# A graph network with layer norm: the norm of four blocks in three turns, and the transposes of a block two turns later

## The chip, the cores and the metric

The kernel runs on one core of a Trainium2 chip. The metric is the device time of one execution in microseconds (us). Three runs of the kernel before gave 4486.59, 4495.84 and 4501.65 us; their median, 4495.84 us, is the time before.

## The reference, cut to what matters

There are 6250 nodes with 256 features and 106,250 edges, sorted by target node (50,000 in both directions, and a loop at each node). Four layers follow each other, each with a layer norm ahead and a residual sum behind:

```
h = LN(x);  h = h + segsum(h[src]);  h = relu(relu(h@W1a+b1a)@W1b+b1b)        # 256 -> 512 -> 512
h = h + segsum(h[src]);  x1 = x + relu(h@W2a+b2a)@W2b+b2b                      # 512 -> 256
x2 = x1 + slice_attention(LN(x1))       # softmax over 64 slices of 8 heads, tokens, attention, back
x3 = x2 + relu(batchnorm(segsum(norm * (LN(x2)@W)[src])))
out = x3 + moe_top2_of_8(LN(x3))
```

`segsum` sums over the edges of each target. All is float32.

## The kernel before

The nodes lie in 49 blocks of 128. Six stages follow one another, each with a barrier between: s0 sorts the edges into tiles and makes the first table, **s1**, **s2** and **s4** are the three that gather (first aggregation with W1a, W1b and W2a; second aggregation with W2b, the layer norm of x1, logits, softmax and token sums; third aggregation with its product, the layer norm of x3, gates and the placing of tokens to experts), s3 is the attention and s5 the experts. The change is in s1, s2 and s4.

In a gathering stage, the edges of a block are tiles of 128, three tiles to a **group**; four blocks have 23 groups (6, 6, 6 and 5), the stage 282 groups and 846 tiles. For each tile GpSimd (POOL) issues one indirect DMA (`Edges.gather`, L280) that fetches 128 rows of a table into a ring of groups: 8 slots in s1, 6 in s2 and s4. Ahead of a group's first gather it waits until TensorE (PE) has counted up `s_used` for the group that held the slot. VectorE (DVE) makes a 128x128 one-hot matrix for each tile (`Edges.onehots`, L295), six groups ahead. PE multiplies the one-hots with the gathered rows and sums up in one of two PSUM banks (`Edges.sums`, L320, and L330 for tiles that belong to two blocks).

Around this each engine walks the same list, `pipeline`. The blocks are cut into **supers** of four (eleven of them, then 2, 2 and 1 blocks). A **turn** is one group. `close(b)` ends a block: DVE adds the block's own rows to the PSUM sum into `agg` (L962, L1188, L1804), in the first turn of the next block (`close_first`); PE transposes `agg` (L990, L1266, L1907), and ScalarE (ACT) copies the transposes (L905, L1133, L1722), both in turn 1 (the second) of the next block. The dense work of a finished super is cut into 22 steps, `piece(s, k)`, that lie beside the turns of the next super: step k is put into turn 2 + k*(n-2)//22 of n turns. In a super of 23 turns these are turns 2, 2, 3, 4, ..., 22. Within a turn the order is: the group's work, `begin`, `close`, and the steps.

Steps touched in s2: products with W2b in steps 0 to 3 (`SECOND`, L1278, added to x1 by DVE at L1198), the layer norm in step 4 (`NORM`, L1202 to L1213, all on DVE: bias, statistics, a reciprocal root of 14 short chained instructions in `rsqrt`, L179 to L185, and four scalings), the transposes of the normed rows in steps 7 to 10 (`TURNED`, PE L1285; ACT copies each at L1141), logits in steps 8 to 11 (L1291), softmax in steps 12 and 13, and transposes and token sums in steps 17 to 20 (`SLICED`, L1298, L1302). In s4: products in 0 to 3 (L1920, L1824), norm in 4 (L1828 to L1838), transposes in 7 to 10 (L1929, L1733), gates in 11, choice in 12, rank in 16, placing in 17 to 21 (L1885, L1886, L1947). In s1 there is no norm: W1a in steps 0 to 3 (L1005), W1b in 5 to 11 (L1011), W2a in 14 to 20 (L1017, L923, L971).

The banks `psT[1]` that take the transposes of the normed rows are single: PE's transposes of block j+1 wait for ACT's copy of block j.

Of the kernel before, what the change touches and what calls it, by code (L numbers as in the profile page):

```python
# [70 lines left out]

SUPER = tuple((b, 4) for b in range(0, 44, 4)) + ((44, 2), (46, 2), (48, 1))
STEPS = 22

TM = (2 * NPAD + NE * (P - 1)) // P
RG = D + NE
# [6 lines left out]
def groups_before(b):  # L83

    return b // UNIT * UG + b % UNIT * GPB


def groups_of(b):

    return groups_before(b + 1) - groups_before(b)  # L90
# [23 lines left out]
def build(nc, a, out):  # L114

    with ExitStack() as whole:
# [70 lines left out]
        def pipeline(group, close, piece, begin=None, close_first=False):  # L187

            for s, (b0, nb) in enumerate(SUPER):
                turns = [(b, g) for b in range(b0, b0 + nb) for g in range(groups_of(b))]  # L190
                for i, (b, g) in enumerate(turns):
                    if g == 0 and b and close_first:
                        close(b - 1)
                    group(b, g)
                    if i == 1 and begin:
                        begin(s)
                    if g == 1 and b and not close_first:
                        close(b - 1)
                    for k in range(STEPS):
                        if s and i == 2 + k * (len(turns) - 2) // STEPS:  # L200
                            piece(s - 1, k)
            close(NB - 1)
            for k in range(STEPS):
                piece(len(SUPER) - 1, k)
# [830 lines left out]
        with ExitStack() as stack:  # L1035
            S = Scope(stack, "s2")
            SECOND, NORM, TURNED, LOGITS = (0, 1, 2, 3), 4, (7, 8, 9, 10), (8, 9, 10, 11)
# [121 lines left out]
            @block.vector  # L1159
            def _(dve):  # L1160
                v = nc.vector
                ch = Chain(dve, s_dve)
                dve.sem_inc(s_evac, 2)
                dve.sem_inc(s_xl, 4)
                dve.sem_inc(s_tok, 4)
                for g in range(GPB):
                    edges.onehots(dve, 0, g)
                v.memset(xl1[:, :, D:D + 1], 1.0)
                rsqrt(ch, dinv[:, :], degree[:, :], dtmp[:, :])
                ch.restart()  # L1170
                dve.wait_ge(s_w, 32)

                def add_spare(k, at):
                    v.tensor_tensor(edges.own[:, :], edges.own[:, :], psM[3][:, :], ALU.add).then_inc(edges.s_oread, 1)

                def group(b, g):
                    if b + 1 < NB and g < groups_of(b + 1):
                        edges.onehots(dve, b + 1, g)
                    if b + 1 < NB and g == groups_of(b) - 1 and groups_of(b + 1) > groups_of(b):
                        edges.onehots(dve, b + 1, g + 1)  # L1180
                    if b == 0 and g == edges.spare_at:
                        edges.spare(dve, add_spare)

                def close(b):
                    s, q = place_of(b)
                    dve.wait_ge(edges.s_used, groups_before(b + 1))
                    dve.wait_ge(s_self, s * 16 + 16)
                    v.tensor_tensor(agg[:, q, :], self_h[:, q, :], psA[b % 2][:, :], ALU.add).then_inc(s_evac, 1)  # L1188

                def piece(s, k):  # L1190
                    b0, nb = SUPER[s]
                    groups = prob[:, 0:nb, :].rearrange("p q (h g) -> p (q h) g", g=G)
                    if k in SECOND[0:nb]:
                        j = SECOND.index(k)
                        if j == 0:
                            dve.wait_ge(s_x[s], 16)
                        dve.wait_ge(s_m2, b0 + j + 1)
                        last = v.tensor_tensor(x1[:, b0 + j, :], x1[:, b0 + j, :], psM[j][:, 0:D], ALU.add)  # L1198
                        if j == nb - 1:
                            ch.link(last)  # L1200
                    if k == NORM:
                        ch.link(v.tensor_tensor(x1[:, b0:b0 + nb, :], x1[:, b0:b0 + nb, :],  # L1202
                                                b2b[:, :].unsqueeze(1).to_broadcast([P, nb, D]), ALU.add))
                        for j in range(nb):
                            last = v.bn_stats(stat[:, j, :], x1[:, b0 + j, :])
                        ch.link(last)
                        for j in range(nb):
                            last = v.bn_aggr(mv[:, j, :], stat[:, j, :])
                        ch.link(last)
                        ch.link(v.tensor_scalar(var[:, 0:nb], mv[:, 0:nb, 1], LN_EPS, None, ALU.add))  # L1210
                        rsqrt(ch, rstd[:, 0:nb], var[:, 0:nb], tmp4[:, 0:nb])
                        for j in range(nb):
                            v.tensor_scalar(xl1[:, j, 0:D], x1[:, b0 + j, :], mv[:, j, 0:1], rstd[:, j:j + 1],  # L1213
                                            ALU.subtract, ALU.mult).then_inc(s_xl, 1)
                        ch.restart()
                    if k in LOGITS[0:nb]:
                        j = LOGITS.index(k)
                        dve.wait_ge(s_lg, b0 + j + 1)
                        last = v.tensor_tensor(prob[:, j, :], psM[j][:, :], slice_b[:, :], ALU.add)
                        if j == nb - 1:  # L1220
                            ch.link(last)
                    if k == SOFTMAX:
                        ch.link(v.tensor_reduce(gmax[:, 0:nb * HEADS], groups, AX, ALU.max))
                        v.tensor_tensor(groups, groups, gmax[:, 0:nb * HEADS].unsqueeze(2).to_broadcast([P, nb * HEADS, G]),
                                        ALU.subtract).then_inc(s_sh, 1)
                    if k == SOFTMAX + 1:
                        dve.wait_ge(s_exp, s + 1)
                        ch.link(v.tensor_reduce(gsum[:, 0:nb * HEADS], groups, AX, ALU.add))
                        ch.link(v.reciprocal(gsum[:, 0:nb * HEADS], gsum[:, 0:nb * HEADS]))
                        v.tensor_tensor(groups, groups,  # L1230
                                        gsum[:, 0:nb * HEADS].unsqueeze(2).to_broadcast([P, nb * HEADS, G]),
                                        ALU.mult).then_inc(s_sw, 1)
                        ch.restart()
                    if k == SOFTMAX + 2:
                        if s == 0:
                            dve.wait_ge(s_wbd, 1)
                            dve.wait_ge(s_ws, 160)
                            for i in range(3):
                                for h in range(2):
                                    rows = slice(h * HD, (h + 1) * HD)  # L1240
                                    v.tensor_copy(wbd[rows, i, rows], wqkv[rows, i, :])
                        dve.wait_ge(s_xl, b0 + nb + 4)
                        v.tensor_tensor(x1[:, b0:b0 + nb, :], x1[:, b0:b0 + nb, :],
                                        bout[:, :].unsqueeze(1).to_broadcast([P, nb, D]), ALU.add)
                    if k == STEPS - 1:
                        for c in range(KH):
                            dve.wait_ge(s_tokp, s * 4 + (c + 1))
                            v.tensor_tensor(tok[:, c, :], tok[:, c, :], psM[c][:, 0:D + 1], ALU.add).then_inc(s_tok, 1)

                pipeline(group, close, piece, close_first=True)  # L1250

            @block.tensor
# [337 lines left out]
        with ExitStack() as stack:  # L1590
            S = Scope(stack, "s4")

            PRODUCT, NORM, TURNED, GATES = (0, 1, 2, 3), 4, (7, 8, 9, 10), 11
# [156 lines left out]
            def _(dve):  # L1750
# [65 lines left out]
                def piece(s, k):  # L1816
# [9 lines left out]
                    if k == NORM:  # L1826
# [5 lines left out]
                        for j in range(nb):  # L1832
                            last = v.bn_aggr(mv[:, j, :], stat[:, j, :])
                        ch.link(last)
                        ch.link(v.tensor_scalar(var[:, 0:nb], mv[:, 0:nb, 1], LN_EPS, None, ALU.add))
                        rsqrt(ch, rstd[:, 0:nb], var[:, 0:nb], tmp4[:, 0:nb])
                        for j in range(nb):
                            v.tensor_scalar(xl3[:, j, 0:D], acc[:, j, :], mv[:, j, 0:1], rstd[:, j:j + 1],  # L1838
                                            ALU.subtract, ALU.mult).then_inc(s_xl, 1)
# [40 lines left out]
                    if k in PLACED[0:nb]:  # L1880
                        j = PLACED.index(k)
                        b = b0 + j
# [336 lines left out]
```

## Time and profile before

| | |
|---|---|
| median of three runs | 4495.84 us |
| the profiled execution's own time | 4527.99 us |
| its span, first to last instruction | 4526.2 us |
| PE, DVE, ACT, POOL busy | 3407.3, 1481.5, 497.8, 2794.2 us |
| mean granted clock of PE | 0.863 |
| gathers of s1 | 71.5 to 1284.7 us |
| gathers of s2 | 1333.4 to 2600.4 us |
| gathers of s4 | 2783.0 to 4009.8 us |

The stages are read one by one, since each has its own ratio of gathers, sums and dense steps. In the views a line such as L320 is the helper in which all three stages sum, so stages are told apart by their stretch of time.

### The profile page before, as it was taken

To read this page: it belongs to the slowest core of one execution; us is meant where nothing else is said; L and a number is where in the kernel's file an instruction comes from. 1 tells how busy PE (TensorE), PEld (TensorE's weight loads), DVE (VectorE), ACT (ScalarE), POOL (GpSimd) and SP (SyncE) were. 2 spreads that over 40 slices of the span, in tenths; PEclk is the share of its full clock that TensorE was granted. 3 is DMA by queue.
4 is the path that set the end of the run, shared out by engine and by line. 5 is a ranking of instruction groups with operands and counts; after the bars stand their busy time and mean duration, and the time that the engine had idled before them with its cause. 6 is when DMAs were issued, how large, how long until landed. Compare 5 with 4: busy or idle time off the path is not lost. (4 is left out here: it accounts for less than half of the span.)

```text
span 4526.2 us, 40559 instructions
## 1 busy us (share of the span) xinstructions
PE 3407.3 (75%) x12357; PEld 2256.3 (50%) x12359; DVE 1481.5 (33%) x5707; ACT 497.8 (11%) x1161; POOL 2794.2 (62%) x2815
## 2 busy tenths in 40 slices
PE   3577777878878889899999976566556656658997
PEld 2354444545453444444444455345444444438986
DVE  5112121212121433444333445234343343442221
ACT  4010000000110000000000002000000000003432
POOL 4666666666646666666666502666666666635664
PEclk7788888988889999999999987777777778769998
DMA  6333333433349666666666527334334333327887
GB/s 199 90 112 112 111 110 110 131 111 111 109 128 330 194 198 200 193 190 194 195 201 205 170 104 240 108 114 123 115 117 128 115 114 114 119 80 174 203 210 188
DMA packets 321341, 687.10 MB, mean 152 GB/s; under 512 B 58976, under 2 KB 148300, under 8 KB 320854
## 3 DMA queue, kind: packets, MB, share of 16 engines
q0 software_dynamic: 169712, 474.01, 37.9%
q10 hardware_dynamic: 86448, 110.35, 7.4%
q1 hardware_dynamic: 64970, 100.14, 6.8%
q8 instruction: 105, 1.72, 0.2%
q14 instruction: 106, 0.87, 0.1%
HBM read 592.43 MB, written 99.13 MB: 153 GB/s over the span
## 5 line engine op out<-in xcount | busy, mean ns | idle before, releaser
L280 POOL DMA_INDIRECT s_edge_rows<-table,w_src_idx x2538 | 2495.4, 983 | 1235.3 <-issue 712.6
L320 PE MATMUL s_psA<-s_edge_rows,s_onehot 128*128 128x257 f32 (+2 forms) x4932 | 1695.0, 487 | 212.1 <-DMA s_edge_rows<-table,w_src_idx 92.3
L320 PEld LDWEIGHTS s_psA<-s_edge_rows,s_onehot 128*128 128x128 f32 x4932 | 1012.6, 210 | 758.6 <-issue 635.1
L295 DVE TENSOR_SCALAR s_onehot<-w_iota_row,w_dst_l 128x128 f32<-128x128 bf16 x2466 | 531.6, 296 | 28.5 <-PEq L149 16.4
L2031 POOL DMA_INDIRECT acc_rows<-s_y,s_tnode x105 | 166.3, 1584 | 130.7 <-DVE s_y L2154 98.8
L1011 PE MATMUL s_psM<-s_h1T,s_w1b 128*128 128x512 f32 (+2 forms) x448 | 195.2, 582 | 52.5 <-ACT s_h1T L913 49.0
L330 PE MATMUL s_psA<-s_edge_rows,s_early 128*128 128x257 f32 (+2 forms) x648 | 221.3, 468 | 10.2 <-issue 9.0
L1017 PE MATMUL s_psM<-s_w2a,s_hT 128*128 128x512 f32 x392 | 196.3, 647 | 22.7 <-issue 16.6
L2179 PE MATMUL s_psU<-s_xT,s_w 128*128 128x128 f32 x1680 | 208.2, 278 | 0.2 <-ACT s_xT L2085 0.2
L2179 PEld LDWEIGHTS s_psU<-s_xT,s_w 128*128 128x128 f32 x1680 | 199.3, 195 | 0.6 <-issue 0.6
L2189 PE MATMUL s_psD<-moe_w,s_hT 128*128 x840 | 199.5, 381 | 0.0
L971 DVE SCALAR_TENSOR_TENSOR s_own<-s_psM,s_eps,s_b2a 128x512 f32<-128x512 f32 x49 | 36.8, 750 | 451.2 <-ACT s_trow L923 313.3
L961 DVE TENSOR_TENSOR w_degree<-w_degree,s_psA 128x1 f32<-128x1 f32 x49 | 7.4, 152 | 513.7 <-remote 294.4
L1947 PE MATMUL moe_psI<-s_at_tile,s_at_lane 128*128 128x392 f32 x196 | 106.5, 678 | 85.9 <-DVE s_at_tile L1886 72.1
L330 PEld LDWEIGHTS s_psA<-s_edge_rows,s_early 128*128 128x128 f32 x648 | 129.6, 200 | 79.7 <-issue 65.9
L1907 PE MATMUL s_psT<-w_ident,s_agg 128*128 128x128 f32 x98 | 26.3, 362 | 180.7 <-DVE s_agg L1804 117.6
L2189 PEld LDWEIGHTS s_psD<-moe_w,s_hT 128*128 128x128 f32 x840 | 152.4, 191 | 16.6
L1011 PEld LDWEIGHTS s_psM<-s_h1T,s_w1b 128*128 128x128 f32 x448 | 89.5, 208 | 134.1 <-issue 77.1
L2154 DVE SCALAR_TENSOR_TENSOR s_y<-s_psD,s_part,s_yb 128x256 f32<-128x256 f32 x105 | 50.8, 484 | 270.5 <-PE s_psD L2189 257.3
L2094 ACT ACTIVATE s_hT<-s_psU,moe_b 128x128 f32<-128x128 f32 x420 | 119.9, 367 | 169.2 <-issue 101.2
L1017 PEld LDWEIGHTS s_psM<-s_w2a,s_hT 128*128 128x128 f32 x392 | 80.3, 209 | 111.3 <-issue 101.8
L2038 POOL DMA_INDIRECT s_xs<-xl_rows,s_tnode x105 | 103.9, 989 | 38.7 <-issue 31.1
(364 smaller groups left out, 2802.6 us busy)
## 6 DMA issues: line engine op xcount, KB each, us to landing
s_w<-in_L_ffn_W_dram SPq DMA_DIRECT2D x105, 512.0 KB
s_edge_rows<-table,w_src_idx POOLq DMA_INDIRECT x2538
s_swT<-swt_rows SPq DMA_DIRECT2D x12, 1024.0 KB
table<-s_trow ACTq DMA_DIRECT2D x11, 1024.0 KB
own_rows<-s_own ACTq DMA_DIRECT2D x11, 1024.0 KB
s_self_h<-own_rows ACTq DMA_DIRECT2D x11, 1024.0 KB
swt_rows<-s_swT ACTq DMA_DIRECT2D x11, 1024.0 KB
extra_rows<-w_zeros SPq DMA_DIRECT2D x7, 896.0 KB
```

Of the source, the lines that this page charges most:

```text
L280: pool.indirect_dma_start(self.rows[:, g % self.SLOTS, t, :], None, self.table, bass.IndirectOffsetOnAxis(ap=src_idx[:, at:at + 1], axis=0 ...
L295: last = nc.vector.tensor_scalar(into[:, t, :], iota_row[:, q * P:(q + 1) * P], dst_l[:, at + t:at + t + 1], None, ALU.is_equal)
L320: last = nc.tensor.matmul(banks[b % 2][:, 0:w], self.onehot[:, g % self.AHEAD, t, :], self.rows[:, g % self.SLOTS, t, col:col + w], start= ...
L330: last = nc.tensor.matmul(banks[(b + 1) % 2][:, 0:w], self.early[:, b % 2, i * GT + t - (CAP - max(EARLY)), :], self.rows[:, g % self.SLOT ...
L1011: last = mm(psM[m][:, 0:n], w1b[:, c, m * P:(m + 1) * P], h1T[:, c, 0:n], start=c == 0, stop=c == KH - 1)
L1017: last = mm(psM[j][:, :], hT[:, c, j * P:(j + 1) * P], w2a[:, c, :], start=c == 0, stop=c == KH - 1)
L1947: mm(psI[:, 0:SLOT_TILES], at_lane[:, (2 * b + i) % 4, :], at_tile[:, (2 * b + i) % 4, :], start=False, stop=False, skip_group_check=True) ...
L2031: pool.indirect_dma_start(acc_rows, bass.IndirectOffsetOnAxis(ap=tnode[:, t:t + 1], axis=0), y[:, t % 4, :], None, compute_op=ALU.add).the ...
L2038: pool.indirect_dma_start(xs[:, t % RING, :], None, xl3_rows, bass.IndirectOffsetOnAxis(ap=tnode[:, t:t + 1], axis=0)).then_inc(s_xs[t % R ...
L2094: last = ac.activation(hT[:, t % 2, m, :], psU[t % 2][:, m * P:(m + 1) * P], ACT.Relu, bias=b1[:, bass.ds(e, 1), m])
L2179: last = mm(psU[t % 2][:, m * P:(m + 1) * P], w1[:, t % WRING, k, m * P:(m + 1) * P], xT[:, t % 2, k, :], start=k == 0, stop=k == KD - 1)
L2189: last = mm(psD[t % 2][:, 0:D], hT[:, t % 2, k, :], w2[:, bass.ds(e, 1), k, :], start=k == 0, stop=k == KH - 1)
```

## The change

```diff
+TURNED_AT = 3
@@ pipeline
-                    if g == 1 and b and not close_first:
+                    if g == TURNED_AT and b and not close_first:
                         close(b - 1)
                     for k in range(STEPS):
-                        if s and i == 2 + k * (len(turns) - 2) // STEPS:
+                        if s and i == TURNED_AT + 1 + k * (len(turns) - TURNED_AT - 1) // STEPS:
                             piece(s - 1, k)
@@ s2 and s4, VectorE's piece, step NORM: statistics stay in it
                         for j in range(nb):
                             last = v.bn_aggr(mv[:, j, :], stat[:, j, :])
                         ch.link(last)
+                    if k == NORM + 1:
                         ch.link(v.tensor_scalar(var[:, 0:nb], mv[:, 0:nb, 1], LN_EPS, None, ALU.add))
                         rsqrt(ch, rstd[:, 0:nb], var[:, 0:nb], tmp4[:, 0:nb])
+                    if k == NORM + 2:
                         for j in range(nb):
                             v.tensor_scalar(xl1[:, j, 0:D], x1[:, b0 + j, :], mv[:, j, 0:1], rstd[:, j:j + 1],
                                             ALU.subtract, ALU.mult).then_inc(s_xl, 1)
```

PE and ACT close a block in turn 3 of the next block instead of turn 1 (DVE still in turn 0). The 22 steps of all three stages begin in turn 4 instead of 2 and end in the same turn as before: in a super of 23 turns, step k lies in turn 4 + 19k//22, so steps 0 and 1 share turn 4, steps 7 and 8 turn 10, and steps 14 and 15 turn 16. The norm's statistics stay in step 4 (turn 7, was 5), the root goes to step 5 (turn 8), the scalings to step 6 (turn 9); the first transposes of normed rows are in turn 10 (were in 8). No instruction is added or removed.

## Rows read from the trace of the kernel before

**Rows 1.** The page: span, and busy time of engines with share and count.

```profile
span 4526.2 us, 40559 instructions
PE 3407.3 (75%) x12357; PEld 2256.3 (50%) x12359; DVE 1481.5 (33%) x5707; ACT 497.8 (11%) x1161; POOL 2794.2 (62%) x2815
```

**Rows 2.** The gather line in s1, s2, s4: count, ns min/median/max, first and last start.

```profile
L280 POOL DMA_INDIRECT s_edge_rows<-table,w_src_idx x846: 951/957/1072, 71.5 to 1284.7; - x170
L280 POOL DMA_INDIRECT s_edge_rows<-table,w_src_idx x846: 951/957/2895, 1333.4 to 2600.4; - x170
L280 POOL DMA_INDIRECT s_edge_rows<-table,w_src_idx x846: 951/957/1993, 2783.0 to 4009.8; - x170
```

**Rows 3.** Stretches: length, busy (x count) of PE, PEld, DVE, ACT, POOL, clock, DMA, GB/s.

```profile
97.00:186.00 89.00, 41.21 (x143) 31.10 (x142) 13.92 (x68) 2.37 (x5) 58.88 (x62) 0.68 0.33 91
386.00:486.00 100.00, 76.26 (x239) 46.21 (x237) 16.92 (x80) 8.12 (x14) 68.44 (x71) 0.88 0.41 116
2062.00:2163.00 101.00, 93.58 (x267) 48.67 (x266) 41.59 (x126) 7.62 (x12) 70.28 (x69) 0.96 0.66 195
3388.00:3488.00 100.00, 63.73 (x245) 48.51 (x244) 39.87 (x176) 3.16 (x9) 68.22 (x71) 0.80 0.40 119
1286.00:1332.00 46.00, 37.54 (x168) 27.04 (x166) 5.56 (x17) 9.88 (x22) 0.00 (x0) 1.00 0.20 62
2602.00:2656.00 54.00, 36.09 (x105) 20.24 (x103) 24.79 (x68) 5.23 (x9) 0.00 (x0) 0.82 0.08 24
4011.00:4060.00 49.00, 22.43 (x71) 15.45 (x70) 24.78 (x125) 1.94 (x6) 0.00 (x0) 0.69 0.11 29
```

**Rows 4.** Timeline in s1: start, us, engine, line, count, idle before it.

```profile
565.44 2.77 PE L320 MATMUL s_psA<-s_edge_rows,s_onehot 128*128 128x257 f32 x12
...
574.54 0.95 POOL L280 DMA_INDIRECT s_edge_rows<-table,w_src_idx  x1 [0.30 <-issue]
579.07 0.60 ACT L923 ACTIVATE s_trow<-s_psM 128x512 f32<-128x512 f32 x1 [20.12 <-DMA x_xl<-in_x_dram]
579.39 0.95 POOL L280 DMA_INDIRECT s_edge_rows<-table,w_src_idx  x1 [3.89 <-remote]
...
580.90 0.69 PE L990 MATMUL s_psT<-w_ident,s_agg 128*128 128x128 f32 x2 [12.70 <-DVE s_agg L962]
```

**Rows 5.** Waits of PE in s1, s2, s4: us in total, times, longest.

```profile
PE s_psT L990 <- DVE s_agg L962: 80.1, 17, 13.3
PE s_psM L1011 <- ACT s_h1T L913: 49.0, 7, 15.7
...
PE s_psT L990 <- issue: 29.0, 8, 8.6
...
PE s_psT L1285 <- ACT s_xl1T L1141: 26.5, 9, 3.8
...
PE s_psT L1266 <- issue: 20.1, 7, 11.0
...
PE s_psT L1907 <- DVE s_agg L1804: 117.6, 14, 18.2
...
PE s_psT L1907 <- issue: 63.1, 7, 20.7
...
PE s_psT L1929 <- ACT s_xl3T L1733: 43.6, 15, 5.9
```

**Rows 6.** Timeline at the end of s2, after the last gather.

```profile
2607.14 2.74 PE L320 MATMUL s_psA<-s_edge_rows,s_onehot 128*128 128x512 f32 x6
...
2607.80 0.69 DVE L1202 TENSOR_TENSOR y_x<-y_x,s_b2b 128x512 f32<-128x512 f32 x1
...
2612.57 0.73 DVE L1213 TENSOR_SCALAR s_xl<-y_x,s_mv,s_rstd 128x256 f32<-128x256 f32 x2
...
2613.04 0.69 PE L1285 MATMUL s_psT<-w_ident,s_xl 128*128 128x128 f32 x2 [3.16 <-DVE s_xl L1213]
...
2614.29 0.66 PE L1285 MATMUL s_psT<-w_ident,s_xl 128*128 128x128 f32 x2 [0.57 <-ACT s_xl1T L1141]
```

More of the change, by code:

```diff
@@ L1834, in piece @@
                         ch.link(last)
+                    if k == NORM + 1:
                         ch.link(v.tensor_scalar(var[:, 0:nb], mv[:, 0:nb, 1], LN_EPS, None, ALU.add))
                         rsqrt(ch, rstd[:, 0:nb], var[:, 0:nb], tmp4[:, 0:nb])
+                    if k == NORM + 2:
                         for j in range(nb):
```

## The prediction, as it was put on record before the changed kernel was run

> **What bounds the kernel now.** I read the page first [rows 1]: PE is busy for 3407.3 of 4526.2 us and POOL for 2794.2, so neither is full over the whole; the stages have to be read singly. Second, the gather line per stage [rows 2]. Each stage issues 846 gathers of 0.957 us, and between two that wait for nothing lie 0.30 us [rows 4], so a stage could issue all in 846 x 1.257 = 1063 us. It takes 1214 (s1), 1268 (s2) and 1228 us (s4): 151, 205 and 165 us are pauses, 521 in all. That is the ground that a change in the order of PE's work can win, and its upper end.
>
> Third, one stretch of about a super per stage [rows 3]. Gathers per us are 0.71 in s1 (71 in 100), 0.68 in s2 (69 in 101) and 0.71 in s4, against 0.80 without pauses. PE is busy for 76, 93 and 64% there. So s2 is bound by PE nearly as much as by gathers, s1 and s4 by the gathers with their pauses. The row that made me careful is the first one: in the first super of s1 no dense steps exist, PE is busy for 46%, and still only 62 gathers are issued in 89 us, 0.70 per us. The pauses don't shrink when PE has little to do.
>
> Fourth, the timeline around one pause [rows 4]. PE's sums of two groups are recorded as over at 568.21. POOL issues until 575.49, has used up its slots and stands for 3.89 us. Then ACT wakes at 579.07 (after 20.12 us), POOL at 579.39, and PE's transposes start at 580.90, after 12.70 us of waiting for DVE's sum. So the others see PE's work late, and see it once POOL has stopped. I don't know why; what matters is what PE can do meanwhile. Here it stands at the close in turn 1, with gathered groups lying ready. The close in turn 3 lets it sum two more groups first.
>
> **The change, part by part. The close two turns later.** Fifth view, PE's waits [rows 5]. At the closes PE idles in s1 for 80.1 + 29.0 = 109 us in 25 times, in s4 for 117.6 + 63.1 = 181 us in 21 times, in s2 for 20.1 us in 7 times. DVE's part stays in turn 0, so two turns of sums move into each wait: 2.8 us in s1 (12 matmuls in 2.77 [rows 4]), about the same or up to double in s4 (clock 0.80), and 5.5 us in s2 (2 x 2.74 [rows 6]). What the filled idle is worth is another matter. In s1 and s4 it counts only as slots given back earlier: two groups more at a pause, so that the next pause comes two groups later. Pauses cost 151/282 = 0.54 us a group in s1 and 0.58 in s4. Upper end: 25 x 2 x 0.54 = 27 us in s1, 21 x 2 x 0.58 = 24 in s4. Lower end: nothing, by the first super. I take half, 13 and 12 us, because at the same late count PE would next stand at another wait (L1011 for ACT has 49.0 us already, L1929 43.6 [rows 5]). In s2 the idle of PE is time itself: up to all 20 us, since two turns of 5.5 us cover the mean wait of 2.9 us; 14 taken, as the longest was 11.0. Sum -39 us.
>
> **Steps in 19 turns instead of 21.** Their total work is unchanged, and they end in the same turn. The products are in turns 4, 4, 5, 6 (were 2, 2, 3, 4): still one turn behind the close, so the wait for ACT's copy of the transposes stays as it is, at nothing. What is new are doubled turns. In turn 10 the transposes of blocks 0 and 1 follow each other, and the second waits for ACT's copy of the first, with no group between. Where the count passes at once, that is 0.57 us [rows 6], with the hand-over about 0.6 us: 11 supers x 0.6 = 7 us in s2, where PE is the bound; in s4 the same 7 us lie under the gathers. The doubled turn 16 of s1 holds products in two different banks and waits for nothing. Softmax and gates move one turn nearer to their users; they have 4 turns, 4 x 2.74 us of sums alone plus steps, and I cost that at nothing. The second end, a late count, is a rival below.
>
> **The norm in three turns.** The same instructions, in turns 7 to 9, where it was turn 5; from the last product (turn 6, was 4) to the first transposes (turn 10, was 8) there are four turns as before. DVE runs these turns without waiting for PE, as the one-hots between them are six groups ahead. It gains what it puts in between, nothing else: three one-hots a turn, which it makes now as well. From the bias sum at 2607.80 to the end of the scalings at 2613.30 are 5.5 us for two blocks [rows 6], some 8 for four with their longer statistics, against four turns of at least 2.74 us. Cost nothing in the body. Without that cover the transposes would wait the 3.16 us that they show in the last block, times 11: 35 us. What the split could give, DVE being free for the one-hots and the close: DVE is busy for 42 of 101 us [rows 3], so nothing as well. No DMA's order is changed; ACT's loads keep their place between `begin` and the first step.
>
> **The ends of the stages.** After the last gather PE's chain alone sets the time, 46, 54 and 49 us [rows 3]. In the last super (6 turns) the steps of the one before lay in turns 2 to 5 and now in 4 and 5. Sums that filled waits of the norm and the softmax come ahead of them: 2 x 2.74 = 5.5 us in s2, 2 x 1.4 = 3 in s4, and 2 in s1, where PE is busy for 82% of the end and little was filled. The supers of 12 and 11 turns have 8 and 7 turns for 22 steps (10 and 9 before), so the norm has one turn less: one sum, 2.7 us, in s2 and 1.5 in s4, some 5 with the rest. Together +15 us. Lower end zero (gathers arrive late anyway), upper end 25.
>
> **Sum.** -13 - 12 - 14 + 7 + 15 = -17 us on 4528.0 us of the profiled execution (span 4526.2 [rows 1]), to 4511. The median of the runs is 0.7% below it; scaled, **4479 us**.
>
> **The rivals.**
> *The pauses are not PE's (same).* The first super speaks for it: 0.70 gathers per us with PE at 46%. Then s1 and s4 give nothing, s2 its 14 less 7, the ends cost 15: +8, **4504**. Against it: in s1 PE stands 12.70 us with slots to give back.
> *All of it, and the clock (faster).* Every wait filled, upper ends 27 + 24 + 20, less 7 + 15: -49. With less idle PE may also keep the higher level: the granted clock in s2 is 0.96, so it runs at 1.2 instead of 2.4 GHz for 8% of the stretch and loses about 4%, 50 us of the stage; a fifth of that may hang on the closes: 10 us more. -59, **4437**.
> The Trainium skill ("TensorE: Matmul & The Clock Gate", the section on what is actually happening) says that the array's clock falls after idling and rises with sustained work. Here the granted clock follows that (0.68 at 46% busy, 0.96 at 93%), and the rule would put the time nearer to this rival; by the rows s1 and s4 would not use a faster PE.
> *The doubled turn strands PE (slower).* PE's second transposes now need, in the same turn, that ACT has seen the first. In rows 4 such a count is seen over 10 us late; at L1285 and L1929 PE has waited for ACT's copies 26.5 us in 9 and 43.6 us in 15 times although a group lay between them [rows 5]. Taking that group away costs up to 2.74 us x 11 = 30 us in s2 and 1.4 x 11 = 15 in s4; with the ends' 15 and half of s2's gain, 14, against: +46 at the outset, and with half of s4's part hidden +39, **4534**. It decides once ACT sees the first transposes later than one group's sums (2.74 us) in most supers.
>
> **How the numbers follow.** Chances: forecast 0.40, pauses not PE's 0.27, all of it 0.12, doubled turn 0.21. About 0.3%, 13.5 us, is what a measurement of this kernel can tell from no change, so the edges are 4482 and 4509. The forecast's own range is 4455 to 4500; six tenths of it lie below 4482 (0.24), the rest is within. The second case lies within for 0.19, above for 0.05 and below for 0.03. The third is faster. The fourth gives 0.18 above and 0.03 within. Faster 0.24 + 0.12 + 0.03 = 0.39; same 0.16 + 0.19 + 0.03 = 0.38; slower 0.05 + 0.18 = 0.23. The range, 4440 to 4522, leaves out half of the third case and the upper half of the fourth.
>
> **What would show it.** Right: PE's waits at L990, L1266 and L1907 fall from 109, 20 and 181 us by at least half; the last gather of s1 and s4 comes some 13 us sooner after the first, s2's some 7; the stretches after the last gather grow by 2, 5 to 8 and 3 to 5 us. The first rival: the same fall of PE's waits, with gather stretches of 1214 and 1228 us as before. The doubled turn: waits at L1285 and L1929 for ACT above 60 us each, with a longer s2. The prediction is wrong as a whole if the gather stretches move by more than 30 us either way, or if the norm's scalings (L1213, L1838) become what L1285 and L1929 wait for.

## The result, and the profile after

The changed kernel takes 4536.8 us (median of 4 runs, 4524.1 to 4541.1), the kernel before, timed beside it, 4495.6 us (4486.6 to 4501.7): ratio 1.0086, interval 1.0069 to 1.0103. It is 0.9% slower; forecast were 4479 us and a range from 4440 to 4522. Single executions of 4634 to 12447 us turned up with several kernels, the one before among them, and no ratio counts them.

The page of the changed kernel, and its gather lines in s1, s2 and s4 (columns as in [rows 1, 2]; the code below the pipeline moved by up to 5 lines, so L280 is L281, L990 L991, L1266 L1269, L1285 L1288, L1298 L1301, L1907 L1912, L1929 L1934):

```profile
span 4522.3 us, 40602 instructions
PE 3412.1 (75%) x12359; PEld 2242.5 (50%) x12359; DVE 1480.6 (33%) x5707; ACT 496.4 (11%) x1161; POOL 2808.4 (62%) x2815
```
```profile
L281 POOL DMA_INDIRECT s_edge_rows<-table,w_src_idx x846: 954/960/1075, 70.9 to 1277.0; - x170
L281 POOL DMA_INDIRECT s_edge_rows<-table,w_src_idx x846: 954/960/2892, 1325.8 to 2585.7; - x170
L281 POOL DMA_INDIRECT s_edge_rows<-table,w_src_idx x846: 954/960/2023, 2769.9 to 4001.1; - x170
```

This one execution is 4 us *shorter* than the one of before [rows 1], while the medians say 41 us longer: the spans of single executions differ by nearly as much as the effect. In the same kernel before, executed again, the span was 4498.2 us instead of 4526.2. So the kernels were run again side by side on one chip, and everything below compares kernels with the kernel before of their own set, by their medians first. After each quoted expectation stands what was measured.

### The profile page after: what moved, and what is told of

Same layout as the page of the kernel before. It is cut to its first block and busy times, and to the rows that moved or that the text cites. A ratio compares the mean times of both kernels' runs of the same rounds, so it can differ in the third digit from the quotient of the medians.

```text
span 4522.3 us, 40602 instructions
## 1 busy us (share of the span) xinstructions
PE 3412.1 (75%) x12359; PEld 2242.5 (50%) x12359; DVE 1480.6 (33%) x5707; ACT 496.4 (11%) x1161; POOL 2808.4 (62%) x2815
## 5 line engine op out<-in xcount | busy, mean ns | idle before, releaser
L281 POOL DMA_INDIRECT s_edge_rows<-table,w_src_idx x2538 | 2509.3, 989 | 1211.1 <-issue 716.1
L1012 PE MATMUL s_psM<-s_h1T,s_w1b 128*128 128x512 f32 (+2 forms) x448 | 189.8, 568 | 16.8 <-ACT s_h1T L914 13.5
L1006 PE MATMUL s_psM<-s_aggT,s_w1a 128*128 128x512 f32 (+2 forms) x224 | 111.1, 642 | 110.3 <-issue 110.3
L1952 PE MATMUL moe_psI<-s_at_tile,s_at_lane 128*128 128x392 f32 x196 | 96.1, 619 | 87.6 <-DVE s_at_tile L1891 50.3
L1012 PEld LDWEIGHTS s_psM<-s_h1T,s_w1b 128*128 128x128 f32 x448 | 86.6, 201 | 97.6 <-issue 74.6
L1934 PE MATMUL s_psT<-w_ident,s_xl 128*128 128x128 f32 x98 | 26.2, 361 | 135.1 <-issue 89.7
```

The source lines that it names most:

```text
L281: pool.indirect_dma_start(self.rows[:, g % self.SLOTS, t, :], None, self.table, bass.IndirectOffsetOnAxis(ap=src_idx[:, at:at + 1], axis=0 ...
L1006: last = mm(psM[m][:, 0:n], w1a[:, c, m * P:(m + 1) * P], aggT[:, c, 0:n], start=c == 0, stop=c == KD - 1)
L1012: last = mm(psM[m][:, 0:n], w1b[:, c, m * P:(m + 1) * P], h1T[:, c, 0:n], start=c == 0, stop=c == KH - 1)
```

## The experiments

Four sets of four kernels, a set on one chip. The first and the last set ran on chips on which the kernel before takes 4495 us, the middle two on chips on which it takes 4083 and 4087 us. I call them pausing and quick; why is told under the quick set.

**One edit of the change at a time (pausing chip).** The kernels before and after again gave ratios 1.0001 (0.9993 to 1.0010) and 1.0088 (1.0073 to 1.0103). Of the changed kernel:

> The changed kernel, unchanged: 1.009 of before, 4530 to 4540 us. Theory A (the doubled turn 10 and the later start of the steps strand PE at L1288 and L1934): its waits there stay near 99 and 135 us (39 and 82 before) and the gather stretches of s2 and s4 are longer than in e1_before by 15 us each. Theory B (the ends of the stages): the gather stretches up to super 11 are the same, and the 40 us lie in the last three supers and after the last gather of each stage.

Measured: the 1.0088 above. Theory A's waits came (L1934 waits 98.1 us, L1288 84.4, shown below), its longer stretches in s2 and s4 did not; they lie where theory B has them. Only the order, that is closes in turn 3, steps from turn 4, the norm whole:

```
-                    if k == NORM + 1:
...
-                    if k == NORM + 2:
```

The same two lines go in s2 and in s4.

> The closes and steps later, the norm whole in one turn (turn 7). If the later closes and steps carry the loss, 1.008 or more. If the split of the norm carries it, 1.000 or faster. By my prediction the split costs nothing, so this is within 5 us of the changed kernel.

Measured: 4539.6 us, ratio 1.0094 (1.0081 to 1.0108). And only the norm in three turns:

```
-TURNED_AT = 3
+TURNED_AT = 1
```

> The norm in three turns (5, 6, 7 in a super of 23 turns), closes in turn 1 and steps from turn 2 as before. The scalings now come after the close in turn 6 on VectorE, which waits for PE's sums of turn 5, and one turn ahead of the first transposes (turn 8). If that is harmless: 1.000. If the normed rows come late: PE's waits for them at L1288 and L1934 rise above 60 us each and the time to 1.005 or more.

Measured: 4483.8 us, 0.9980 (0.9970 to 0.9989). The split is worth 0.2% here; the order carries the whole loss.

Where does it lie? I cut each stage in two: supers 1 to 10, and "the end", from the first gather of super 11 to the next stage's first gather (s2 and s4: to the stage's last matmul). The windows of the kernel before and of the changed one on this chip; first three rows supers 1 to 10 of s1, s2, s4, then the three ends (columns as in [rows 3]):

```profile
169.70:1153.00 983.30, 759.95 (x2369) 469.04 (x2370) 196.65 (x877) 90.52 (x157) 665.24 (x691) 0.87 0.40 112
1420.30:2439.30 1019.00, 921.29 (x2675) 480.69 (x2674) 412.22 (x1262) 79.50 (x127) 709.99 (x690) 0.96 0.67 199
2864.00:3849.20 985.20, 604.09 (x2189) 457.08 (x2190) 384.22 (x1699) 32.19 (x90) 673.52 (x691) 0.78 0.40 119
...
1153.00:1323.00 170.00, 143.19 (x516) 93.97 (x514) 31.12 (x122) 25.75 (x51) 84.20 (x88) 0.94 0.38 109
2439.30:2637.50 198.20, 165.93 (x507) 92.07 (x505) 82.13 (x232) 19.34 (x32) 87.27 (x87) 0.92 0.47 141
3849.20:4031.30 182.10, 115.03 (x375) 81.07 (x374) 83.66 (x385) 6.95 (x20) 83.96 (x87) 0.73 0.31 91
```
```profile
165.80:1151.50 985.70, 774.17 (x2367) 476.02 (x2367) 196.68 (x877) 90.38 (x158) 665.07 (x690) 0.86 0.40 112
1433.80:2446.40 1012.60, 927.83 (x2678) 480.58 (x2678) 412.92 (x1262) 79.27 (x127) 708.90 (x691) 0.96 0.68 201
2888.60:3874.90 986.30, 619.75 (x2170) 468.91 (x2170) 377.67 (x1658) 31.70 (x90) 674.45 (x690) 0.77 0.40 119
...
1151.50:1336.60 185.10, 147.06 (x518) 95.93 (x516) 31.24 (x122) 25.75 (x51) 84.00 (x88) 0.92 0.34 100
2446.40:2662.90 216.50, 167.81 (x507) 93.91 (x505) 82.09 (x232) 19.23 (x32) 87.58 (x87) 0.88 0.43 130
3874.90:4063.90 189.00, 109.11 (x379) 80.25 (x379) 88.99 (x417) 6.83 (x20) 84.62 (x87) 0.70 0.30 87
```

The ten full supers moved by +2.4, -6.4 and +1.1 us, the ends by +15.1, +18.3 and +6.9: 40 us, while the span grew by 35. One pair of traces proves little, so I took the same windows from all ten traces of pausing chips. With the short supers' steps as before, the three ends together take 544 to 556 us (five traces), with late steps 583 to 598 (four); the thirty full supers take 2972 to 3011 us and 2983 to 2993, and there the change can't be seen. (A kernel with DVE's long operations cut up, the last run below, takes 2964 there and is not counted.) That also settles the first pair of traces: its ends grew by 27 us, and its full supers happened to be 28 us shorter. PE's waits changed all the same. Before (us in total, times, longest; whole trace):

```profile
PE s_psT L1907 <- DVE s_agg L1804: 164.6, 21, 16.2
...
PE s_psT L1266 <- DVE s_agg L1188: 64.2, 10, 16.9
...
PE s_psT L1929 <- issue: 51.0, 12, 9.9
PE s_psT L990 <- DVE s_agg L962: 48.5, 14, 11.6
```

and in the changed kernel:

```profile
PE s_psT L1934 <- issue: 98.1, 19, 11.1
PE s_psT L1288 <- DVE s_xl L1216: 84.4, 13, 13.1
...
PE s_psM L1012 <- ACT s_h1T L914: 31.8, 8, 12.7
...
PE s_psT L991 <- DVE s_agg L963: 11.8, 5, 2.9
```

The closes hardly wait any more: L1912 (L1907 before) has 2.3 us left, s1's L991 has 11.8. The waits stand at the next instructions that need another engine: L1288, L1934, L1012. A pause is passed on, not filled.

**Ends against full supers, closes against steps (quick chip).** Short supers are the last three (12, 11 and 6 turns). All four kernels have the norm in three turns. First the change in the full supers alone:

```
+                at = TURNED_AT if len(turns) == 23 else 1
-                    if g == TURNED_AT and b and not close_first:
+                    if g == at and b and not close_first:
-                        if s and i == TURNED_AT + 1 + k * (len(turns) - TURNED_AT - 1) // STEPS:
+                        if s and i == at + 1 + k * (len(turns) - at - 1) // STEPS:
```

> The change as it is in the eleven supers of 23 turns; in the last three (12, 11 and 6 turns) the closes go back to turn 1 and the steps to turn 2 on. Theory (the ends of the stages carry the loss: supers 11 to 13 and the stretch behind them were 42 us longer in the changed kernel, the eleven full supers 7 us shorter): ratio 0.998 to 1.000, 4485 to 4495 us. Rival (the doubled turn 10 and the late steps strand PE in every super): it stays at 1.006 or above, 4522 us. If both hold in part: between, 1.002 to 1.005.

Measured: 4101.3 us against 4083.1, 1.0043 (1.0030 to 1.0056): between the two accounts. In the short supers alone (`at = 1 if len(turns) == 23 else TURNED_AT`):

> The opposite: closes in turn 1 and steps from turn 2 in the eleven supers of 23 turns, closes in turn 3 and steps from turn 4 in the last three alone; the norm in three turns everywhere. Theory (ends): the whole loss is here, 4484 for the split alone and about 40 more, 4515 to 4530, ratio 1.005 to 1.008. Rival (doubled turn in every super): ratio below 1.001, as the split alone.

Measured: 4112.9 us, 1.0069 (1.0056 to 1.0082). Late closes (three of four blocks) with early steps:

```
-                    if g == TURNED_AT and b and not close_first:
+                    if g == (1 if b == b0 else TURNED_AT) and b and not close_first:
-                        if s and i == TURNED_AT + 1 + k * (len(turns) - TURNED_AT - 1) // STEPS:
+                        if s and i == 1 + 1 + k * (len(turns) - 1 - 1) // STEPS:
```

> Closes in turn 3 where the closed block is not the last of the super before (3 of 4), in turn 1 where it is; the steps of the super before stay where they were, from turn 2 on. Norm in three turns. Theory (it is the steps, pushed together at the ends, and not the closes): as the split alone, ratio 0.996 to 1.000, with PE's waits at the closes of the full supers gone by two thirds. Rival (the late close itself costs, as slots or the buffers of the sums come free later for DVE and ACT): 1.004 or above. By my prediction's terms for the closes it would be 25 to 30 us faster than the split alone, 4455; I no longer believe that, since the pauses of POOL came as often in every kernel run.

Measured: 4086.6 us, 1.0007 (0.9997 to 1.0017). Early closes (`g == 1`) with late steps:

> All closes in turn 1 as before; the steps from turn 4 on, in 19 turns, as in the changed kernel, with the doubled turn 10. Norm in three turns. Theory (steps crowded behind the last gathers): the whole loss is here, ratio 1.006 to 1.010, 4522 to 4540 us, and PE waits at the closes as long as before. Rival (the closes carry it): ratio 0.996 to 1.000.

Measured: 4115.0 us, 1.0073 (1.0060 to 1.0086). So on this chip late closes alone cost nothing and bring nothing. Late steps carry the loss, and they do so in the short supers: 1.0073 with late steps in all supers is hardly more than the 1.0069 of the short ones alone. What the full supers add, 0.3 to 0.4% that my theory did not have, comes only with closes and steps both late; where it lies is shown under the next set.

**The anchors on a quick chip.** The kernel before: 1.0001 (0.9993 to 1.0010).

> The changed kernel. Theory (the loss is the steps crowded around the last gathers, and hangs on no pause of POOL): on either chip 30 to 50 us slower than the kernel before, on the quick one ratio 1.008 to 1.011, with the last three supers and what follows them carrying at least 30 us. Rival (the loss comes with the late counts and the pauses): on a chip without pauses within 10 us of the kernel before, ratio below 1.0025.

Measured: 4127.1 us against 4087.3, 1.0101 (1.0087 to 1.0116): the same 40 us.

> Norm in three turns, closes and steps as before. It was 0.2% quicker than before where POOL pauses (0.998). Theory (it gives back PE's late waits for DVE in s2): with no pauses no gain, ratio 0.999 to 1.001. Rival (it shortens what DVE itself has to do ahead of the sums): 0.998 on any chip.

Measured: 4090.8 us, 1.0009 (1.0000 to 1.0018). The split's gain was seen on the pausing chip only. Counted from the split alone, the two halves of the set before add up to the whole: 0.0060 for the ends and 0.0034 for the full supers, against 0.0092.

What makes this chip quick shows in POOL's waits, of the kernel before on the pausing chip and then here:

```profile
POOL s_edge_rows L280 <- issue: 714.6, 2319, 2.1
POOL s_edge_rows L280 <- PE s_psA L320: 149.9, 101, 6.4
...
POOL s_edge_rows L280 <- remote: 117.7, 37, 5.5
...
POOL s_edge_rows L280 <- DMA s_spare_dst<-dst_pad: 96.0, 42, 4.1
```
```profile
POOL s_edge_rows L280 <- issue: 746.9, 2452, 0.3
...
POOL s_edge_rows L280 <- PE s_psA L320: 30.4, 69, 6.3
```

The pauses are all but absent: of POOL's idle time ahead of gathers other than "issue" and the first one, 41 us are left of 462. POOL issues as fast as it can, a full super of s1 takes 88 us and not 98. The same windows as above, kernel before and changed kernel:

```profile
150.70:1027.80 877.10, 730.70 (x2397) 458.11 (x2397) 197.48 (x871) 93.65 (x159) 666.93 (x691) 0.96 0.45 126
1260.70:2184.70 924.00, 905.02 (x2697) 474.53 (x2696) 414.82 (x1262) 79.97 (x128) 713.83 (x690) 1.00 0.74 223
2587.80:3467.00 879.20, 574.36 (x2197) 421.02 (x2197) 385.53 (x1700) 32.14 (x90) 669.01 (x691) 0.90 0.45 133
...
1027.80:1171.50 143.70, 127.43 (x477) 85.96 (x475) 26.69 (x106) 24.32 (x48) 84.21 (x88) 0.98 0.44 129
2184.70:2370.00 185.30, 158.09 (x485) 87.54 (x483) 82.54 (x232) 18.26 (x30) 87.50 (x87) 0.93 0.51 151
3467.00:3619.60 152.60, 97.75 (x355) 69.77 (x353) 77.40 (x362) 6.58 (x19) 84.29 (x87) 0.81 0.38 108
```
```profile
150.30:1027.80 877.50, 733.89 (x2390) 464.98 (x2391) 197.45 (x871) 93.32 (x159) 667.27 (x691) 0.94 0.45 126
1266.60:2191.00 924.40, 903.14 (x2690) 473.42 (x2689) 417.23 (x1262) 78.95 (x128) 714.25 (x690) 1.00 0.74 223
2606.70:3497.20 890.50, 588.39 (x2199) 433.34 (x2198) 382.37 (x1700) 33.16 (x91) 680.33 (x691) 0.88 0.45 132
...
1027.80:1177.50 149.70, 129.52 (x481) 86.79 (x479) 26.84 (x107) 24.69 (x49) 84.62 (x88) 0.97 0.42 124
2191.00:2391.60 200.60, 162.99 (x495) 90.89 (x494) 82.68 (x232) 18.54 (x31) 87.52 (x87) 0.91 0.47 140
3497.20:3656.50 159.30, 96.75 (x356) 72.20 (x354) 77.82 (x362) 6.46 (x19) 84.70 (x87) 0.79 0.36 104
```

Ends: +6.0, +15.3, +6.7 = +28 us. In the eight traces of quick chips the three ends together take 480 to 483 us with early steps in the short supers and 510 to 513 with late ones. Full supers: +0.4, +0.4, +11.3, and in s4 POOL's busy time grew by the same 11.3 us for the same 691 gathers. Gathers got longer, not rarer. In all eight traces supers 1 to 10 of s2, and those of s4, take POOL's busy time there plus 210 us, whatever PE does, and though PE is busy for 98% of the time in s2. Counted from the split alone (917.0 and 885.5 us) they grew by 7.5 us in s2 and 5.0 in s4: that is the 0.3% of the full supers. The set before shows it too: in s2 POOL is busy for 713 us with closes and steps both late, and for 704 us with only one of them late, and the stretch is 9 us longer.

Where do the ends grow? Behind the last gather by 5.6, 5.9 and 6.3 us here, and by 3.3, 7.0 and 5.6 on the pausing chip. The rest, 10 and 24 us, lies between the first and the last gather of the short supers: here nearly all of it in s2, in the gathers of the super of 11 turns (57.8 to 67.0 us, and 62.3 to 72.0 on the pausing chip). POOL issues them while PE, up to six groups behind, is still in the super of 12 turns.

PE's idle time in the ends (length less busy) goes from 16 to 20 us in s1, from 27 to 38 in s2, and from 55 to 63 in s4; in s2 its busy time grows by 5 us too. Four of PE's waits in the end of s2, the kernel before and then the changed one; the first two of each lie in the super of 12 turns, the others in that of 6:

```profile
2220.98 0.44 PE L1285 MATMUL s_psT<-w_ident,s_xl 128*128 128x128 f32 x2 [0.22 <-DVE s_xl L1213]
...
2247.70 1.11 PE L1298 MATMUL s_psT<-w_ident,s_prob 128*128 128x128 f32 x4 [7.26 <-DVE s_prob L1230]
...
2327.33 0.69 PE L1285 MATMUL s_psT<-w_ident,s_xl 128*128 128x128 f32 x2 [3.16 <-DVE s_xl L1213]
...
2341.97 0.66 PE L1298 MATMUL s_psT<-w_ident,s_prob 128*128 128x128 f32 x4 [2.04 <-DVE s_prob L1230]
```
```profile
2238.26 0.69 PE L1288 MATMUL s_psT<-w_ident,s_xl 128*128 128x128 f32 x2 [5.78 <-DVE s_xl L1216]
...
2266.44 1.11 PE L1301 MATMUL s_psT<-w_ident,s_prob 128*128 128x128 f32 x4 [6.82 <-DVE s_prob L1233]
...
2348.16 0.69 PE L1288 MATMUL s_psT<-w_ident,s_xl 128*128 128x128 f32 x2 [5.74 <-DVE s_xl L1216]
...
2361.76 0.66 PE L1301 MATMUL s_psT<-w_ident,s_prob 128*128 128x128 f32 x4 [4.61 <-DVE s_prob L1233]
```

In the super of 12 turns the steps of a full super, four blocks, now lie in 8 turns and not in 10. From the last product with W2b (turn 5, was 3) to the first transposes of normed rows (turn 6, was 5) PE has one group's sums to do, where it had two, and its wait for the norm grows by 5.6 us. The wait for the softmax, long before as well, does not. In the super of 11 turns the steps of two blocks lie in 7 turns instead of 9, and on this chip neither kernel waits there for norm or softmax for more than 0.6 us. In the last super, where 22 steps lie in two turns and not in four, both waits grow, by 2.6 us each. These four make up the 10 us of idle time that s2's end gained. The 5 us of busy time and the waits of s1 and s4 I have not taken apart.

The other direction (`at = 1 if len(turns) == 23 else 0`):

> As the split alone, but in the last three supers the closes lie in turn 0 and the steps from turn 1 on, one turn earlier than before. Theory (the later the steps of a short super lie, the longer its end: two turns later cost about 30 us): one turn earlier gives some back, 0.996 to 0.999 of before, 5 to 15 us. Rival (the loss came from crowding alone, which is over at 9 and 10 turns): same as the split alone. A close in turn 0 can also wait for DVE's sum with nothing in front of it, three times a stage: up to 5 us lost.

Measured: 4088.3 us, 1.0001 (0.9992 to 1.0011), within the noise of the split alone.

**Dose, and the stretched gathers (pausing chip).** The changed kernel with s4's two long adds cut up, L1831 as here and L1804 alike:

```
+                        for j in range(nb):
+                            last = v.scalar_tensor_tensor(acc[:, j, :], acc[:, j, :], 0.0, xrow[:, j, :], ALU.max, ALU.add)
+                        ch.link(last)
```

> The changed kernel with DVE's two adds of 128x1024 in s4 (L1804 and L1831, 1.2 us each, both inputs in SBUF) cut into one of 128x256 per block. On a chip without POOL's pauses: theory (a gather that meets such an add waits for its end): the stretched gathers of s4 go, its eleven full supers fall by 6 to 11 us, and the time by as much, ratio to the kernel before about 1.008 instead of 1.0101. Rival (DVE's four adds hold POOL as long as one, or the stretch is chance): s4 as in the changed kernel, ratio 1.010. On a chip with pauses both say 1.008 to 1.009, since a stretched gather only moves the next pause.

Measured: 4542.0 us against 4495.6, 1.0097 (1.0077 to 1.0117). The chip was of the pausing kind, where both accounts say the same, so it does not tell them apart. TURNED_AT = 2:

> Closes in turn 2 and steps from turn 3 on (half of the shift), norm in three turns. Theory (the ends get longer with every turn by which the steps are pushed together): about half of the loss, 15 to 25 us, ratio 1.004 to 1.006. Rival (the loss starts only where three or more steps share a turn with nothing between): the short supers of 12 and 11 turns are still below three a turn mostly, ratio below 1.003.

Measured: 4507.9 us, 1.0024 (1.0015 to 1.0033). Against the split alone (0.9980, first set) one turn costs 0.44% and two 1.08%: it grows faster than in proportion, nearer to the rival's account. In its trace the three ends take 563 us, between the 544 to 556 and the 583 to 598 above.

Early ends in s1 and s4 alone (`ends=0` for their pipelines):

> Norm in three turns; full supers as before; in the last three supers of s1 and s4 the closes lie in turn 0 and the steps from turn 1, in s2 as before. From the run with all three stages early: ends of s1 3 us and of s4 9 us shorter, s2's 5 us longer, which is now left out. Theory (the dose holds on the early side too): 8 to 14 us below the split alone, ratio 0.997 to 0.999 on a chip without pauses, 0.995 to 0.997 on one with. Rival (the 8 us shorter span was chance, as the medians were equal): ratio 1.000 to 1.001, or 0.998 with pauses.

Measured: 4488.9 us, 0.9980 (0.9970 to 0.9990): the split's gain and nothing more. The rival was right: more turns for the steps than the kernel before gives them bring nothing. With the long operations cut too, s4's adds as above and s2's softmax thus (the multiplication alike):

```
+                        for j in range(nb):
+                            hs = slice(j * HEADS, (j + 1) * HEADS)
+                            last = v.tensor_tensor(groups[:, hs, :], groups[:, hs, :], gmax[:, hs].unsqueeze(2).to_broadcast([P, HEADS, G]), ALU.subtract)
+                        last.then_inc(s_sh, 1)
```

> The same, with s4's two adds cut per block as above and, in s2, the softmax's subtraction and multiplication of 128x2048 (2.3 us each, in which gathers of up to 2.9 us are seen) cut into four of 128x512. Theory (gathers wait for DVE's long operations on two tensors): on a chip without pauses the stretched gathers of s2 fall from about 45 us to 15, of which PE (idle for 13 us in ten supers of s2) lets through 5 to 10, and s4 gives 6 more: ratio 0.993 to 0.996. Rival (cutting changes nothing): as the run without it.

Measured: 4479.3 us, 0.9962 (0.9949 to 0.9975): 16 us less than before, the fastest kernel of the study. The expectation was written for a chip without pauses, and the interval overlaps that of the run without the cut (0.9970 to 0.9990), so the times alone don't prove that the cut helps; the windows speak for it. Supers 1 to 10 of s2, without the cut and then with it (POOL's busy time is the fifth of those with a count):

```profile
1425.50:2429.70 1004.20, 924.90 (x2676) 475.89 (x2675) 412.26 (x1262) 79.29 (x126) 705.81 (x691) 0.98 0.68 202
```
```profile
1417.80:2411.80 994.00, 926.14 (x2680) 479.96 (x2679) 416.37 (x1319) 78.83 (x126) 677.26 (x690) 0.97 0.69 204
```

POOL is busy for 28.6 us less, and the stretch is 10 us shorter; it is the shortest of all ten traces of pausing chips, whose others have 1002 to 1027 us.

## Why the prediction was wrong, step by step

The spans grew by 35 us where -17 was forecast. Of these 52 us, 29 are gains in the full supers that did not come, and 25 are ends that cost more.

- **The closes later, -13 and -12 in s1 and s4: wrong.** The waits did go, as the first sign asked: L990's and L1907's 48.5 and 164.6 us for DVE, with 36 and 41 more put down to "issue", became 11.8 and 2.3. The full supers did not shorten (+2.4, +1.1 us, within the scatter of the traces). The step that failed is "counts as slots given back earlier": filling the wait at the close did not move the next pause; PE waited elsewhere instead. The first rival, that the pauses are not PE's, had this right, and its evidence stood in the first row of [rows 3]. I gave half of the upper end a place in the sum against that row. What does set the pauses stays open, and late closes by themselves ran only on a quick chip (1.0007).
- **The closes in s2, -14: not shown as a gain of the closes.** Supers 1 to 10 shortened by 6.4 us, but with the split alone the stretch from the first gather to super 11 fell from 1116.3 to 1099.5 us with the closes in turn 1. PE's wait moved from L1266 to L1288.
- **The doubled turn, +7: right in size, but without a price.** On the quick chip PE waits 10 times, 5.7 us, at L1288 for ACT in supers 1 to 10 of s2, 0.57 us each, as in [rows 6]; late steps alone left that stretch at 914.6 us, as early ones did (914.3). "PE is the bound" was wrong there. The rival with its 39 us is wrong too: its sign, over 60 us of waiting for ACT at each of L1285 and L1929, reads 1.7 and 13.0 us in the second trace of the changed kernel (L1288 and L1934), and at most 44.3 in the first. That its 4534 us is 3 us from the measured time is luck.
- **The norm split, 0: nearly.** 0.1% lost on the quick chip, at the edge of the noise, and 0.2% gained on the pausing one. Why it gains there was not tested.
- **The ends, +15, upper end 25: the failed term.** They cost 40 us on the pausing chip and 28 on the quick one. The part behind the last gathers was about right: 16 and 18 us where the signs had 10 to 15. What was mis-sized is the short supers themselves, "some 5 with the rest": 24 us on the pausing chip, 10 on the quick one. I treated those of 12 and 11 turns alike. The quick chip showed in its place that it is the one of 12 turns, which still carries the steps of four blocks, where PE's wait for the norm grows (0.22 to 5.78 us, where I had counted one sum of 2.7 us), and that the gathers of the next super, which follow PE, take 9 us longer. In s1 the gathers of the short supers take 134 to 136 us in three of the four traces with late ends on pausing chips and 121 to 127 in the fourth and in all others; on quick chips they take 109 us in every kernel. So this part goes with the pauses, and why it comes is open.
- **The level, -0.7%.** I scaled a span of 4526.2 us; the same kernel gave 4498.2 later, its eleven full supers of s2 8 us shorter (1124.1 and 1116.3 us).

- **The faster rival: wrong.** PE is busier in the ten full supers (s1 by 14 us, s4 by 16) for the same work, the granted clock stayed at 0.96 in s2 and went from 0.87 to 0.86 in s1, and nothing came of it.

Corrected sum for the pausing chip, from the windows: full supers +2.4 - 6.4 + 1.1, ends +40.3, all else -2.3: +35.1 us in the spans, +40 in the medians.

## What to carry to other kernels

A schedule written as k * (turns) // steps shrinks hardest where there are few turns. Price such a shift in each short pass by itself, and first in the one that carries a full pass's work in few turns: count there what is left between an instruction and the step that waits for it. If a stretch with an idle engine keeps the rate of the loaded one, no gain may be put down to giving that engine more to do. And measure the kernel before twice, on more than one chip if one can, before building on a single trace.

## What the runs showed of the hardware

**Two kinds of chip.** The same kernel takes 4495 us in the first timing and in two of the sets, and 4083 to 4087 us in the two others, with the same gather (957 to 960 ns, 0.30 us between two). What differs in the traces is that on the first kind another engine acts late on PE's work while POOL issues, until POOL has used up its slots (12.70 us in [rows 4]): PE's waits for DVE at L1907 are 164.6 us there and 1.0 on the quick kind. Why is open. Both kinds gave the change the same 40 us.

**A gather waits for DVE's operation on two tensors.** POOL's timeline in s2 of the kernel before, quick chip, and DVE's beside it (start, us, engine, line, count, idle before it):

```profile
1789.65 0.96 POOL L280 DMA_INDIRECT s_edge_rows<-table,w_src_idx  x1 [0.30 <-issue]
1790.92 0.96 POOL L280 DMA_INDIRECT s_edge_rows<-table,w_src_idx  x1 [0.30 <-issue]
1792.18 2.61 POOL L280 DMA_INDIRECT s_edge_rows<-table,w_src_idx  x1 [0.30 <-issue]
```
```profile
1789.37 2.27 DVE L1223 TENSOR_REDUCE s_gmax<-s_prob 128x32 f32<-128x2048 f32 x1
1791.67 2.29 DVE L1224 TENSOR_TENSOR s_prob<-s_prob,s_gmax 128x2048 f32<-128x2048 f32 x1
```

Two gathers beside the reduction, which reads one tensor, take 0.96 us; the one that starts while L1224 runs, which reads two, ends 0.83 us after it. The whole of s2 in this trace says the same of DVE's operations of 0.9 us or more on two tensors in SBUF. 44 gathers start while one of them runs: 42 are stretched to over 1.2 us, each ending 0.83 us after it, and the two others had 0.31 us or less of it left. Of 21 gathers that had started first, one is stretched. 46 gathers meet only a reduction, and none is.

The Trainium skill says so ("SBUF — State Buffer", the section on two separate sides): an operation of VectorE with two inputs in SBUF and a GpSimd operation that reads SBUF, as a gather reads its row numbers, need a port pair that they share; the one that starts first has it for its whole instruction, and the other waits. The trace agrees, the order of starting included, and it shows no such wait beside L1223 or L1228.

Which gather meets which operation depends on the phase between DVE and POOL, and so moving DVE's norm by some turns moved s4 by 11 us. In supers 1 to 10 POOL's busy time was 669.0 us in the kernel before, 675.3 with the split alone, 680.3 in the changed kernel, for 691, 690 and 691 gathers. In all of s4, 5, 15 and 19 stretched gathers had started while such an operation ran, and 1, none and 4 had not. No run moved the phase alone: the one meant to cut s4's two operations on such a chip fell on the other kind. In s2, cutting the two operations of 2.29 us took 28.6 us from POOL, as shown above.
